# Attention of a cross-attention and expert layer: keys moved to the partitions, scores computed twice, work ordered by batch

## The chip, the cores and the metric

One NeuronCore of a Trainium2 chip. The metric is device time in microseconds (us) of one launch. All times here are of executions of the same program on the same inputs.

## What is computed

The input x has 4 batches of 512 tokens of width 128, the context 4 batches of 77 keys. The second half is a layer with eight experts, of which each token takes the two best. Cut to what matters:

```python
q = (layernorm(x) @ Wq + bq).reshape(b, nq, 16, 8).transpose(0, 2, 1, 3)
k = (ctx @ Wk + bk).reshape(b, nk, 16, 8).transpose(0, 2, 1, 3)
v = (ctx @ Wv + bv).reshape(b, nk, 16, 8).transpose(0, 2, 1, 3)
scores = jnp.where(mask, -jnp.inf, jnp.einsum('bhqd,bhkd->bhqk', q, k) / np.sqrt(8))
attn = jnp.einsum('bhqk,bhkd->bhqd', jax.nn.softmax(scores, -1), v)
x = x + attn.transpose(0, 2, 1, 3).reshape(b, nq, 128) @ Wo + bo
z = layernorm(x)
probs = softmax(z @ router_w + router_b)          # 9 choices: 8 experts, identity
gates = the two largest probs, 0 elsewhere
y = einsum('ebtf,efd->ebtd', gelu(einsum('btd,edf->ebtf', z, w1)), w2)
x = x + einsum('bte,ebtd->btd', gates[..., :8], y) + gates[..., 8:] * z
```

## The kernel before

Every instruction is placed by hand on its engine. Each engine runs its own list in order and waits on counting semaphores, so what stands behind a waiting instruction waits too. Everything is float32; a float32 product shows as two records on PE, a transpose as one. There are four parts.

1. **Start.** SP and ACT load the inputs. PE projects the keys (L724) and values (L728). DVE puts keys into kT and values into v_sb (L1019 to L1032). PE repeats V over the keys of all heads (L754), DVE masks it into vbd (L1139).
2. **Attention**, 16 tiles of 128 tokens, four in a batch, `n` the batch and `t` the tile. Tokens lie on the partitions, the 16 x 77 = 1232 keys of all heads on the free axis. For a tile, PE makes the scores in four groups of 32 rows (L774, four heads in each, 308 columns) into the four banks of ps_s. DVE reads each half of ps_s twice, for the maximum (L1058) and to subtract it (L1062). ACT takes the exponential of all 1232 columns (L665). PE transposes the result in ten chunks (L798), ACT copies them out (L547), and PE multiplies them with vbd (L807), 99 columns each; the row sums come along as a ninth column of each head. DVE divides by them (`weigh`, L1081, L1082), PE transposes (L782) and projects (L786), DVE adds the residual and takes statistics (`residual`, L1070 to L1076). The tiles overlap: the lists run `attend` of tile i-1 and `attn_t` of tile i-2 in step i.
3. **Router**, once a batch, within the steps of the next one: ACT normalizes (`norm2`, L591), PE transposes (L840) and makes the logits (L849), DVE picks the two best (`choose`, L1092 to L1107), PE counts the tokens of each expert (`ranks`, L861 to L867), DVE turns these into slots (`place`, L1116 to L1128), POOL sends the rows to DRAM by eight indirect DMAs (`send`, L480). The last batch is split in a part of three tiles and a part of one. Then DVE makes tables (from L1189), SP and ACT write padding rows, and SP waits for all sends.
4. **Experts**, 40 tiles of gathered rows: PE L917, L926 and L935, ACT L701, DVE L1208 to L1222, POOL L523. Then the pairs of results are added and stored.

Batches 1 and 2 are two rounds of a hardware loop, with registers in the waits; batches 0 and 3 are written out. The transposes' banks ps_t are taken in a numbered order of 18 "fills" a batch (`FILLS`, `ORDER`).

## Time and profile before

| | us |
|---|---|
| median of 3 timed runs | 253.03 (250.68 to 253.9) |
| span of the profiled execution | 257.3 |

The profiled execution has no time of its own beside its span. Its span is 4.3 us above the median of the timed runs, so it stands as its own time, and a sum made on it is brought to the median by taking 4.3 us off.

PE is busy for 191.6 us of the span, DVE 156.0, ACT 102.0, POOL 102.4. In the profile, L12 is line 12 of the kernel. PE is the matmul side of TensorE and PEld its weight loads. A row of a timeline gives start and duration in us, engine, line, operation, output and inputs, and count; in brackets stands how long the engine was idle before, and what released it. Ends of matmuls are modelled. PEclk is the granted share of TensorE's clock; where the trace holds no record of the clock, it shows as 1.00.

### The profile page before, as it was taken

The numbers are of one execution on the slowest core, as the hardware profiler recorded it, in microseconds if no ns is written. First come the engines' busy times: TensorE is split into PE (matmuls) and PEld (weight loads), VectorE is DVE, ScalarE is ACT, GpSimd is POOL, SyncE is SP. The second block draws the span as 40 slices with busy tenths as digits, with TensorE's granted clock in tenths as the row PEclk, the third lists the DMA queues.
The fourth block names the chain that finished last, engine by engine and source line by source line (L and its number), as shares of the span: only waits on it lengthen the run. The fifth ranks groups of instructions, "written<-read, shape, count | busy, mean of one in ns | idle before, by whom it ended". The sixth has DMA issues, their size and how long they took to land.

```text
span 257.3 us, 5658 instructions
## 1 busy us (share of the span) xinstructions
PE 191.6 (74%) x1467; PEld 169.9 (66%) x1468; DVE 156.0 (61%) x498; ACT 102.0 (40%) x210; POOL 102.4 (40%) x148
## 2 busy tenths in 40 slices
PE   1747899999986599849783200999999999999500
PEld 0516488778765587739782100899999999999500
DVE  2799968788883678938853650254554554554226
ACT  2411565678654476436653310122322322323100
POOL 8293001002047520782057479044554554554600
PEclk9999999999999589997978555599999999999955
DMA  3535892000001000110001031212222222210069
GB/s 98 159 122 215 263 309 83 4 0 0 4 20 44 9 0 0 37 36 0 0 28 50 21 103 50 61 47 74 59 68 64 71 62 68 62 52 11 3 218 271
DMA packets 20303, 18.30 MB, mean 71 GB/s; under 512 B 3255, under 2 KB 16752, under 8 KB 20287
## 3 DMA queue, kind: packets, MB, share of 16 engines
q1 hardware_dynamic: 16831, 13.98, 18.5%
q0 software_dynamic: 2304, 3.75, 4.7%
q10 hardware_dynamic: 1152, 0.37, 0.6%
q8 instruction: 8, 0.13, 0.2%
q14 instruction: 8, 0.07, 0.1%
HBM read 10.60 MB, written 8.50 MB: 74 GB/s over the span
## 4 chain that ended last, share of the span: by engine, by line
PE 48%; DVE 23%; issue 9%; DMA 6%; ACT 4%; another core or an unknown queue 4%; SPq 3%; POOL 1%; DVEq 0%; POOLq 0%; ACTq 0%
PE ps_s L926 14%; PE ps_av L807 8%; PE ps_av L935 7%; PE ps_o L935 6%; PE ps_t L798 5%; DVE mx L1058 4%; DVE sc L1062 3%; DMA pair_sb<-pairs 2%; PE ps_t L917 2%; DMA ctx_sb<-in_ctx 2%; DVE v_sb L1030 1%; PE ps_s L774 1%; DVE v_sb L1032 1%; SPq L317 1%
## 5 line engine op out<-in xcount | busy, mean ns | idle before, releaser
L523 POOL DMA_INDIRECT pairs<-yg,xg x40 | 39.1, 976 | 44.1 <-issue 22.7
L701 ACT ACTIVATE hT<-ps_s 128x512 f32<-128x512 f32 x40 | 23.9, 597 | 61.5 <-PE ps_s L926 61.5
L480 POOL DMA_INDIRECT slots<-rows,slot x32 | 31.7, 990 | 39.1 <-issue 18.3
L926 PE MATMUL ps_s<-xgT,w_now 128*128 128x128 f32 x320 | 44.4, 283 | 0.0
L807 PEld LDWEIGHTS ps_av<-vbd,exT 128*128 128x128 f32 x320 | 40.9, 205 | 2.4 <-issue 2.4
L807 PE MATMUL ps_av<-vbd,exT 128*128 128x99 f32 (+1 forms) x320 | 41.8, 286 | 0.8 <-issue 0.8
L926 PEld LDWEIGHTS ps_s<-xgT,w_now 128*128 128x128 f32 x320 | 40.5, 199 | 0.1
L1215 DVE COPY w_now<-w_sb 128x512 f32 x40 | 17.2, 429 | 21.5 <-issue 16.9
L798 PE MATMUL ps_t<-ident,ex 128*128 128x128 f32 x160 | 28.1, 314 | 0.1
L547 ACT COPY exT<-ps_t 128x384 f32<-128x384 f32 (+1 forms) x48 | 24.1, 514 | 7.5 <-PE ps_t L798 4.2
L1058 DVE TENSOR_REDUCE mx<-ps_s 128x8 f32<-128x616 f32 x32 | 25.4, 793 | 2.5 <-PE ps_s L774 1.9
L1062 DVE TENSOR_TENSOR sc<-ps_s,mx 128x616 f32<-128x616 f32 x32 | 25.6, 799 | 1.3
L665 ACT ACTIVATE ex<-sc 128x1232 f32<-128x1232 f32 x16 | 19.7, 1230 | 10.2 <-DVE sc L1062 10.1
L436 POOL TENSOR_TENSOR kbd<-kT,hm 128x308 f32<-128x308 f32 x4 | 2.8, 704 | 51.9 <-PE ps_s L774 46.8
L798 PEld LDWEIGHTS ps_t<-ident,ex 128*128 128x128 f32 x160 | 20.9, 160 | 2.6 <-ACT ex L665 0.8
L917 PE MATMUL ps_t<-ident,xg 128*128 128x128 f32 x40 | 11.5, 287 | 14.6 <-DMA xg<-slots 14.5
L935 PE MATMUL ps_av<-w_sb,hT 128*128 x160 | 22.2, 283 | 0.0
L935 PE MATMUL ps_o<-w_sb,hT 128*128 x160 | 21.5, 277 | 0.2 <-issue 0.2
L935 PEld LDWEIGHTS ps_av<-w_sb,hT 128*128 128x128 f32 x160 | 20.2, 198 | 0.2
L935 PEld LDWEIGHTS ps_o<-w_sb,hT 128*128 128x128 f32 x160 | 19.5, 192 | 0.4 <-issue 0.4
L774 PE MATMUL ps_s<-kbd,qT 32*128 32x308 f32 x128 | 16.7, 510 | 2.9 <-DVE sc L1062 1.6
L1208 DVE COPY xgT<-ps_t 128x128 f32<-128x128 f32 x40 | 11.4, 284 | 8.3 <-PE ps_t L917 8.3
(157 smaller groups left out, 239.9 us busy)
## 6 DMA issues: line engine op xcount, KB each, us to landing
xg<-slots SPq DMA_DIRECT2D x40, 65.0 KB
pairs<-zeros SPq DMA_DIRECT2D x4, 512.0 KB, 4.0
w_sb<-in_L_ffn_w SPq DMA_DIRECT2D x1, 2048.0 KB, 9.7
pair_sb<-pairs SPq DMA_DIRECT2D x3, 512.0 KB, 4.7
x_sb<-in_x SPq DMA_DIRECT2D x4, 256.0 KB, 6.7
out<-out_sb SPq DMA_DIRECT2D x3, 256.0 KB, 2.9
pairs<-yg,xg POOLq DMA_INDIRECT x40
slots<-rows,slot POOLq DMA_INDIRECT x32
```

Of the source, the lines that this page charges most:

```text
L480: pool.indirect_dma_start(slots, bass.IndirectOffsetOnAxis(ap=slot[k][:, t, c:c + 1], axis=0), rows[:, t, :], None, bounds_check=ROWS - 1, ...
L523: pool.indirect_dma_start(pairs, bass.IndirectOffsetOnAxis(ap=xg[:, u, D + 1:D + 2].bitcast(U32), axis=0), yg[:, u % 4, :], None, bounds_c ...
L547: act.copy(dst, src).then_inc(t_used, 1)
L665: act.activation(ex[:, t % 2, 0:HK], sc[:, t % 2, :], ACT.Exp).then_inc(ex_ready, 1)
L701: act.activation(hT[:, u % 2, :], ps_h[u % 2], ACT.Gelu).then_inc(h_used, 1)
L774: m = pe.matmul(ps_s[:, g, 0:GK], qT[r, P * t:P * (t + 1)], kbd[r, :, :].rearrange("p h k -> p (h k)"), start=True, stop=True)
L798: m = pe.transpose(ps_t[bank][:, P * (c - a):P * (c - a + 1)], ex[:, par, P * c:P * (c + 1)], ident[:, :])
L807: m = pe.matmul(ps_av[:, (DH + 1) * head0[c]:(DH + 1) * head0[c] + VC], exT[:, par, P * c:P * (c + 1)], v, start=c == 0, stop=c == NCH - 1 ...
L926: m = pe.matmul(ps_h[par][:, P * c:P * (c + 1)], w1_now[:, par, P * c:P * (c + 1)], xgT[:, par, :], start=True, stop=True)
L935: m = pe.matmul(ps_y[par], hT[:, par, P * c:P * (c + 1)], w2_sb[:, bass.ds(e + P * c, D)], start=c == 0, stop=c == FC - 1)
L1058: link(dve.tensor_reduce(m, s, AX.X, ALU.max))
L1062: dve.tensor_tensor(o.rearrange("p (g h k) -> p g h k", g=2, k=NK), s, m.rearrange("p (g h) -> p g h", g=2).unsqueeze(3) .to_broadcast([P, ...
```

## The change

Part 2 is written anew, and with it the order of parts 1 and 3. Part 4 is the same, but for the PSUM banks that it uses. The loop over batches is unrolled, and so are the registers in waits.

- **Scores twice.** The scores of a tile are made as before (`scores`, same shapes), but only for their maximum: DVE reads each half once (`maxima`) and puts the 16 maxima of a token into spare columns of mpad. After the four tiles of a batch, PE transposes mpad (`shifts_t`, four transposes), and DVE adds the maxima as extra rows to two masked copies of q (`shift_q`, two instructions of 512 columns), which POOL prepares (`own_q`). The second product (`scores_t`) has the keys on the partitions and 512 tokens on the free axis. Its stationary side kaug holds -1 in the extra rows, so that the product is the score less the maximum. The 308 keys of a group go in three pieces, of 128, 103 and 77 partitions, each with four products (one for each group of 32 rows) into the four banks of ps_s.
- **Exponential straight into place.** ACT takes it from PSUM, two banks (1024 columns) at a time, six times a batch (`exps`). Its output is the right-hand side of the next product: the ten transposes a tile and the copies exT are gone.
- **V stationary.** `attend` multiplies V (32 columns, one product for each of four column groups, 512 tokens) into ps_a, and a block of ones (`onest`) in the same way into ps_b, which gives the row sums on all partitions of a head: 24 products a batch. `weigh` is one reciprocal and one product of 128x512, and the result is already transposed for Wo: `attn_t` and its copy are gone.
- **By batch.** Projection, residual, statistics and normalization run once for 512 tokens. The router's part for batch n-2 runs in step n; the last batch isn't split. Scores of the next batch wait for the last exponentials, since ps_s is shared. The normalization and q of batch n+1 stand in front of the exponentials of batch n on ACT, those of batch 1 behind the exponentials of batch 0.
- **Start.** V is masked by two instructions of DVE instead of six; it is repeated only for the first two pieces (four products of PE in `spread_v`, two of them of 512 columns), and masked into vst and onest by six instructions (`spread`).

Cut to its core:

```diff
+    PIECE = [(NK, NK + P), (NK + P, GK), (0, NK)]
+    ROWSOF = [z - a for a, z in PIECE]
+    NC3 = len(PIECE)
+    SHIFT_ROW = 23
...
+            def spread_k(n):
+
+                k = kT[:, n * NK:(n + 1) * NK].unsqueeze(1).to_broadcast(by_block)
+                pool.tensor_tensor(kbd[:, n], k, hm4[:, :].unsqueeze(2).to_broadcast(by_block),
                                    ALU.mult).then_inc(kbd_ready, 1)
...
+            def shift_k(n):
+
+                pool.wait_ge(kbd_ready, n + 1)
+                pool.tensor_tensor(kaug[:, n], kbd[:, n], sm4[:, :].unsqueeze(2).to_broadcast(by_block),
+                                   ALU.subtract).then_inc(kaug_ready, 1)
+
+            def own_q(n):
+
+                pool.wait_ge(q_ready, n + 1)
+                if n >= 2:
+                    pool.wait_ge(sT_full, 6 * (n - 1))
+                pool.tensor_tensor(qa[n % 2][:, :], qT[n % 2][:, :], own_a[:, 0:1].to_broadcast([P, S]),
+                                   ALU.mult).then_inc(qown_ready, 1)
+                pool.tensor_tensor(qb[n % 2][:, :], qT[n % 2][:, :], hm4[:, 0:1].to_broadcast([P, S]),
+                                   ALU.mult).then_inc(qown_ready, 1)
...
+            def exps(n, c):
+
+                for pair in range(2):
+                    act.wait_ge(sT_full, n * 6 + c * 2 + pair + 1)
+                    if n > 0:
+                        act.wait_ge(av_full, (n - 1) * NC3 + c + 1)
+                    k = ROWSOF[c]
+                    act.activation(eT[c][0:k, 2 * pair:2 * pair + 2, :], ps_s[0:k, 2 * pair:2 * pair + 2, :],
+                                   ACT.Exp).then_inc(ex_ready, 1)
...
+                    norm2(n - 2)
+                    store_x2nT(n - 2)
+                if 0 < n < B - 1:
+                    store_xn(n + 1)
+                    store_xnT(n + 1)
+                    store_q(n + 1)
+                exps(n, 0)
+                exps(n, 1)
+                if n == 0:
+                    act.wait_ge(stats1_ready, B)
+                    seeds(seed1[:, TT:NT], mv1[:, TT:NT, 1], 2, seed1_ready)
+                if n >= 2:
+                    router_exp(n - 2)
+                exps(n, 2)
+                if n == 0:
+                    act.wait_ge(shift1_ready, 2)
+                    store_xn(1)
+                    store_xnT(1)
+                    store_q(1)
+                if n >= 1:
...
+            def spread_v():
+
+                pe.wait_ge(repeat_ready, 2)
+                pe.wait_ge(kT_ready, 1)
                 pe.wait_ge(v_ready, 1)
-                begin_fill(PRE_V)
...
+                for c, bank in enumerate((ps_a, ps_b)):
+                    k = ROWSOF[c]
+                    pe.matmul(bank[0:k, :], repeat[:, P * c:P * c + k], v_sb[:, :, :].rearrange("k b d -> k (b d)"),
+                              start=True, stop=True)
+                    i = pe.matmul(ps_m[1][0:k, B * c:B * (c + 1)], repeat[:, P * c:P * c + k], validT[:, :],
                                   start=True, stop=True)
...
+            def shifts_t(n):
+
+                if n == 0:
+                    pe.wait_ge(vr_used, 1)
+                if n >= 2:
+                    pe.wait_ge(x2nT_ready, n - 1)
+                pe.wait_ge(s_used, (n + 1) * TT * 2)
+                for t in range(TT):
+                    i = pe.transpose(ps_m[1][:, P * t:P * (t + 1)], mpad[:, t, :], ident[:, :])
+                i.then_inc(mT_full, 1)
+
+            def scores_t(n, c):
+
+                a, z = PIECE[c]
+                q = (qb if c == 2 else qa)[n % 2]
+                if c == 0:
+                    pe.wait_ge(kaug_ready, n + 1)
+                    pe.wait_ge(aug_ready, 2 * n + 2)
+                for pair in range(2):
+                    if c > 0 and pair == 0:
+                        pe.wait_ge(ex_ready, n * 6 + 2 * c)
+                    for g in (2 * pair, 2 * pair + 1):
+                        r = slice(32 * g, 32 * g + 32)
+                        m = pe.matmul(ps_s[0:z - a, g, :], kaug[r, n].rearrange("p h k -> p (h k)")[:, a:z], q[r, :],
+                                      start=True, stop=True)
+                    m.then_inc(sT_full, 1)
+
+            def attend(n, c):
+
+                k = ROWSOF[c]
+                if c == 0:
+                    if n == 0:
+                        pe.wait_ge(vr_used, 2)
+                    else:
+                        pe.wait_ge(at_ready, n)
+                pe.wait_ge(ex_ready, n * 6 + 2 * c + 2)
+                for g in range(G):
+                    r = slice(32 * g, 32 * g + 32)
+                    pe.matmul(ps_a[r, :], vst[0:k, c, n * D + 32 * g:n * D + 32 * g + 32], eT[c][0:k, g, :],
+                              start=c == 0, stop=c == NC3 - 1)
+                for g in range(G):
+                    r = slice(32 * g, 32 * g + 32)
+                    m = pe.matmul(ps_b[r, :], onest[0:k, c, n, :], eT[c][0:k, g, :], start=c == 0,
+                                  stop=c == NC3 - 1)
+                m.then_inc(av_full, 1)
+
+            def project(n):
+
+                pe.wait_ge(aug_ready, 2 * n + 4 if n + 1 < B else 2 * n + 2)
+                if n == B - 1:
+                    pe.wait_ge(x2nT_ready, n)
+                pe.wait_ge(at_ready, n + 1)
+                for t in range(TT):
+                    i = pe.matmul(ps_m[1][:, D * t:D * (t + 1)], attnT[:, P * t:P * (t + 1)], wo_sb[:, :],
+                                  start=True, stop=True)
+                i.then_inc(o_full, 1)
...
+            for n in range(B):
+                if n > 0:
+                    scores(n, 0)
+                    attend(n - 1, 2)
+                scores(n, 1)
+                scores(n, 2)
+                if n >= 2:
+                    norm2_t(n - 2)
+                if 0 < n < B - 1:
+                    norm1_t(n + 1)
+                scores(n, 3)
+                if 0 < n < B - 1:
+                    project_q(n + 1)
+                if n >= 2:
+                    logits(n - 2)
+                shifts_t(n)
+                scores_t(n, 0)
+                if n > 0:
+                    project(n - 1)
+                scores_t(n, 1)
+                attend(n, 0)
+                if n >= 2:
+                    ranks(n - 2)
+                scores_t(n, 2)
+                attend(n, 1)
+                if n == 0:
+                    norm1_t(1)
+                    project_q(1)
+            attend(B - 1, 2)
+            norm2_t(B - 2)
+            logits(B - 2)
+            project(B - 1)
+            ranks(B - 2)
+            norm2_t(B - 1)
+            logits(B - 1)
+            ranks(B - 1)
...
+            def spread(c, values, own):
+
+                k = ROWSOF[c]
+                head = piecehead[0:k, c, :]
+                dve.tensor_tensor(vst[0:k, c, :].rearrange("p (x j d) -> p x j d", j=HG, d=DH),
+                                  values.rearrange("p (x j d) -> p x j d", j=HG, d=DH),
+                                  head.unsqueeze(1).unsqueeze(3).to_broadcast([k, B * G, HG, DH]), ALU.mult)
+                return dve.tensor_tensor(onest[0:k, c, :, :].rearrange("p b (j d) -> p b j d", d=DH),
+                                         own.unsqueeze(2).unsqueeze(3).to_broadcast([k, B, HG, DH]),
+                                         head.unsqueeze(1).unsqueeze(3).to_broadcast([k, B, HG, DH]), ALU.mult)
...
+            def maxima(n, t):
+
                 for half in range(2):
...
+                    if n > 0 and t == 0 and half == 0:
+                        dve.wait_ge(mT_full, n)
+                    dve.tensor_reduce(mpad[:, t, :].rearrange("p (g r) -> p g r", g=G)
+                                      [:, 2 * half:2 * half + 2, SHIFT_ROW:SHIFT_ROW + HG],
+                                      ps_s[:, 2 * half:2 * half + 2, 0:GK].rearrange("p g (h k) -> p g h k", k=NK),
+                                      AX.X, ALU.max).then_inc(s_used, 1)
+
+            def shift_q(n):
+
+                dve.wait_ge(mT_full, n + 1)
+                dve.wait_ge(qown_ready, 2 * n + 2)
+                dve.scalar_tensor_tensor(qa[n % 2][:, :], ps_m[1][:, :], shift_a[:, 0:1], qa[n % 2][:, :],
+                                         ALU.mult, ALU.add).then_inc(aug_ready, 1)
+                dve.scalar_tensor_tensor(qb[n % 2][:, :], ps_m[1][:, :], sm4[:, 0:1], qb[n % 2][:, :],
+                                         ALU.mult, ALU.add).then_inc(aug_ready, 1)
+
+            def weigh(n):
+
+                dve.wait_ge(av_full, NC3 * (n + 1))
+                link(dve.reciprocal(inv[:, :], ps_b[:, :]))
+                if n > 0:
+                    dve.wait_ge(o_full, n)
+                dve.tensor_tensor(attnT[:, :], ps_a[:, :], inv[:, :], ALU.mult).then_inc(at_ready, 1)
...
+            maxima(0, 0)
+            dve.wait_ge(piece_ready, 3)
+            spread_all()
+            for n in range(B):
+                for t in range(TT):
+                    if n > 0 or t > 0:
+                        maxima(n, t)
+                shift_q(n)
+                if n == 0:
+                    for b in range(1, B):
+                        stats1(b)
                     refine1(slice(TT, NT), 2)
-                    spread_v()
-                if t == 2 and kind == "first":
-                    dve.wait_ge(xb_ready, B)
-                if t == 3 and kind != "first":
-                    choose(n - 1)
-                if kind != "first" or t >= 2:
-                    i_ = residual(i - 2, (t + 2) % 4)
-                    if t == 1:
-                        i_.then_inc(stats_ready, 1)
-                if kind != "first" or t >= 1:
-                    weigh(i - 1, (t + 1) % 2)
-                if t == 1 and kind != "first":
+                    constants()
+                if n > 0:
+                    weigh(n - 1)
+                if n >= 2:
+                    choose(n - 2)
+                if n > 0:
+                    residual(n - 1)
+                if n >= 2:
+                    place(n - 2)
+                if n > 0:
                     refine2(n - 1)
-                if t == 3 and kind != "first":
-                    place(n - 1)
-
-            def steps():
-                for t in range(TT):
-                    step("first", 0, t)
-                chain_at = chain.local
-                with dve.Fori(1, B - 1) as n:
-                    chain.enter(n - 1, LINKS)
-                    for t in range(TT):
-                        step("mid", n, t)
-                    chain.leave(B - 2)
-                for t in range(TT):
-                    step("last", B - 1, t)
-
-            steps()
-            residual(NT - 2, 2).then_inc(stats_ready, 1)
+            weigh(B - 1)
+            choose(B - 2)
+            residual(B - 1)
+            place(B - 2)
             refine2(B - 1)
-            weigh(NT - 1, 1)
-            residual(NT - 1, 3).then_inc(stats_ready, 1)
             choose(B - 1)
-            refine2(B)
             place(B - 1)
```

**PE, a tile of batch 1 or 2 before**: scores, transpose of the attention, transposes of the exponentials in ps_t, projection, products with vbd.

```order
L774 MATMUL ps_s<-kbd,qT 128x308 x4
L782 MATMUL ps_o<-ident,av 128x128
L798 MATMUL ps_t<-ident,ex 128x128 x7
L786 MATMUL ps_o<-wo_sb,avT 128x128
L798 MATMUL ps_t<-ident,ex 128x128 x3
L807 ISA
L807 MATMUL ps_av<-vbd,exT 128x99
```

The last row comes ten times, with register instructions between. **PE now, in the step of batch 2**, from the transposed product of its first piece on (kaug the keys with the extra rows, eT the exponentials, vst and onest V and the ones):

```order
L664 MATMUL ps_m<-ident,mpad 128x128 x4
L679 MATMUL ps_s<-qa,kaug 128x512 x4
L709 MATMUL ps_m<-wo_sb,attnT 128x128 x4
L679 MATMUL ps_s<-qa,kaug 103x512 x4
L694 MATMUL ps_a<-eT,vst 32x512 x4
L698 MATMUL ps_b<-eT,onest 32x512 x4
```

The projection of the batch before stands between the first and the second piece. Ahead of it, in the same step, stand the scores of the four tiles and what was placed between them:

```order
L652 MATMUL ps_s<-kbd,qT 128x308 x4
L694 MATMUL ps_a<-eT,vst 32x512 x4
L698 MATMUL ps_b<-eT,onest 32x512 x4
L652 MATMUL ps_s<-kbd,qT 128x308 x8
L718 MATMUL ps_m<-ident,rows_0 128x128 x4
L615 MATMUL ps_m<-ident,xn_sb 128x128 x4
L652 MATMUL ps_s<-kbd,qT 128x308 x4
L621 MATMUL ps_m<-xnT,wq_sb 128x512
L729 MATMUL ps_m<-wr_sb,x2nT 128x64 x4
```

The two transposes, of batch 0's normalized rows and batch 3's, stand ahead of the fourth tile's scores, which wait behind them. **DVE now, in the step of batch 2**, from the maxima to the start of choosing:

```order
L960 TENSOR_REDUCE mpad<-ps_s 128x2x4 x8
L969 SCALAR_TENSOR_TENSOR qa<-ps_m,shift_a,qa 128x512
L971 SCALAR_TENSOR_TENSOR qb<-ps_m,sm,qb 128x512
L977 RECIPROCAL inv<-ps_b 128x512
L980 TENSOR_TENSOR attnT<-ps_a,inv 128x512
L1005 TENSOR_TENSOR lgx<-ps_m,rb_sb 128x4x9
```

The eight reductions stand alone, without the subtractions between them. The reciprocal and the product behind it are ahead of what PE needs for the projection.

## Rows read from the trace of the kernel before

**Rows 1.** Busy time by stretch: start, attention (two), its end, tables and sends.

```profile
core 0: us, PE busy (x) PEld busy (x) DVE busy (x) ACT busy (x) POOL busy (x), PEclk, DMA share, GB/s
0.00:46.00 46.00, 32.26 (x178) 23.89 (x183) 35.16 (x100) 18.64 (x38) 16.24 (x45) 1.00 0.57 175
46.00:71.00 25.00, 24.17 (x208) 19.88 (x205) 21.09 (x69) 18.54 (x41) 1.52 (x4) 1.00 0.01 2
71.00:125.90 54.90, 44.37 (x340) 38.05 (x339) 39.60 (x107) 30.56 (x64) 24.10 (x33) 0.91 0.05 17
125.90:147.70 21.80, 10.32 (x70) 8.80 (x68) 11.79 (x82) 9.07 (x29) 10.26 (x11) 0.73 0.09 29
147.70:161.70 14.00, 0.68 (x2) 0.42 (x3) 4.11 (x16) 1.28 (x1) 11.24 (x16) 0.50 0.26 74
```

**Rows 2.** Waits: engine and line, released by: us in total, times, longest.

```profile
DVE rsum L1081 <- remote: 9.9, 2, 5.9
```

**Rows 3.** The chain that ended last, in order of time: start, us, what.

```profile
80.26 5.39 another core or an unknown queue
...
110.65 4.01 another core or an unknown queue
...
156.18 1.57 DMA slots<-padrows
```

**Rows 4.** Groups by line and shape, DVE: busy us, mean ns, idle before.

```profile
L1062 DVE TENSOR_TENSOR sc<-ps_s,mx 128x616 f32<-128x616 f32 x32 | 25.6, 799 | 1.3
L1058 DVE TENSOR_REDUCE mx<-ps_s 128x8 f32<-128x616 f32 x32 | 25.4, 793 | 2.5 <-PE ps_s L774 1.9 <-issue 0.3
...
L1032 DVE TENSOR_SCALAR v_sb<-v_sb,validT 77x128 f32<-77x128 f32 x4 | 7.3, 1879 | 0.0
...
L1081 DVE RECIPROCAL rsum<-ps_av 128x16 f32<-128x16 f32 x16 | 3.9, 243 | 14.7 <-remote 9.9 <-PE ps_av L807 4.5
...
L1019 DVE SCALAR_TENSOR_TENSOR kT<-ps_av,bk_sb,valid 128x308 f32<-128x308 f32 x1 | 0.5, 504 | 0.0
...
L1117 DVE RECIPROCAL lsum<-lsum 128x3 f32<-128x3 f32 x1 | 0.2, 176 | 0.0
```

**Rows 5.** Groups by line and shape, ACT.

```profile
L547 ACT COPY exT<-ps_t 128x384 f32<-128x384 f32 x32 | 15.3, 478 | 6.2 <-PE ps_t L798 3.0 <-remote 1.9 <-issue 0.2
...
L547 ACT COPY exT<-ps_t 128x512 f32<-128x512 f32 x16 | 9.4, 586 | 1.3 <-PE ps_t L798 1.1
```

**Rows 6.** Timeline, PE: query projection (first, at the start), scores, products.

```profile
12.58 2.05 PE L742 MATMUL ps_t<-xnT,wq_sb 128*128 128x512 f32 x2 [0.77 <-ACT xnT L547]
...
43.27 1.05 PE L742 MATMUL ps_t<-xnT,wq_sb 128*128 128x512 f32 x2
...
48.22 2.37 PE L807 MATMUL ps_av<-vbd,exT 128*128 x20
50.52 0.80 PE L774 MATMUL ps_s<-kbd,qT 32*128 32x308 f32 x8
```

**Rows 7.** Timeline, DVE and ACT: first and last of choose, of place; a normalization.

```profile
65.56 0.19 DVE L1092 TENSOR_TENSOR lgx<-lg_sb,rb_sb 128x36 f32<-128x36 f32 x1
...
67.50 0.20 DVE L1107 TENSOR_TENSOR lgx<-lgx,top 128x44 f32<-128x44 f32 x1
...
69.30 0.18 DVE L1116 TENSOR_REDUCE lsum<-lex 128x4 f32<-128x36 f32 x1
...
70.45 0.23 DVE L1128 TENSOR_REDUCE slot<-prod 128x8 uint32<-128x72 f32 x1
...
75.43 1.63 ACT L565 ACTIVATE xn_sb<-x_sb,shift,rstd 128x128 f32 x4
```

**Rows 8.** Timeline, the sends' last stretch and the first expert product.

```profile
144.66 0.97 POOL L480 DMA_INDIRECT slots<-rows,slot  x1 [3.85 <-ACT rows L577]
...
153.78 0.97 POOL L480 DMA_INDIRECT slots<-rows,slot  x1 [0.30 <-issue]
...
161.74 0.42 PE L926 MATMUL ps_s<-xgT,w_now 128*128 128x128 f32 x1
```

821 lines of the change are left out of this document (288 added, 533 removed).

## The prediction

> **What bounds the kernel now.** I read busy time by stretch first [rows 1]. The reader is to see that DVE is busy for 21.1 of the 25 us of batch 1 (46 to 71) and PE for 24.2: both are near their limit there. In the next 54.9 us, two batches, both have slack (39.6 and 44.4), and the list of waits [rows 2] shows part of why: DVE waited twice, 9.9 us together, for a semaphore whose sender the profile doesn't know. The chain that ended last has the same two places, 5.39 and 4.01 us [rows 3]. In both, products were done by the record and their signal came late. I call these 9.4 us the late signals. Without them a batch takes 23 to 25 us, set by DVE with PE close behind. After the attention come 21.8 us in which no engine is busy for more than 12: a chain of small steps for the last batch's router; then 14.0 us of tables and sends, and the experts.
>
> **Durations.** They come from one profiled execution, whose span is 257.3 us; the median of the runs shown is 253.0, so a sum on the span loses 4.3 at the end.
> - DVE: maximum of a half 0.79, subtraction of a half 0.80 [rows 4]. A two-source instruction of 512 columns: from 504 ns at 308 columns and 793 to 799 at 616, some 0.95 ns a column, so 0.70 us.
> - ACT: a copy takes 478 ns for 384 columns and 586 for 512 [rows 5], 0.84 ns a column, so an exponential of 1024 columns 1.02 us. Four normalizations take 1.63 [rows 7].
> - PE: the query projection of 512 columns is two records and takes 1.05 with its fill [rows 6]; I take 0.44 a record. The 20 products of 128 by 99 take 2.37, so about 0.11 a record of some 100 to 128 columns. The eight records of the scores, 308 columns in four row groups, take 0.80; one after another they would be 8 x 0.26 = 2.1. So row groups run side by side, and a transposed product of four row groups, 512 columns, is 2 x 0.44 + 0.2 = 1.1.
> - Choosing takes 2.1 from its first to its last row, placing 1.4 [rows 7]. Residual and statistics for 512 tokens I put at 2.2 (0.7, and eight short instructions like those of choosing), the four chained steps of the second normalization at 0.8 after their seed.
>
> **Two prices that no row shows.** The reciprocal of 128x512: the trace has 176 ns for 3 columns and 243 for 16 [rows 4], so 5.2 ns a column. Bounds: 0.7 us, if the 16 columns are slow only for their stride and it runs like other instructions, and 3.8, if the longest of the 16 (0.26) sets the slope. I take 0.18 + 509 x 0.0052 = 2.9, the line through both rows. The Trainium skill, VectorE: DVE Perf Modes, section on the fixed hardware budget, says that the reciprocal is an iterative divide with a repeat count of 8. At its 0.96 GHz and eight cycles an element that would be an estimated 4.3 us, and the sum would be 5 us longer; the slope of the rows is below it, so the trace doesn't fully agree.
>
> The product of four column groups (`attend`): no row has any. If they run side by side as row groups do, 2 x 2 x 0.44 + 0.2 = 2.0 us for both banks; if one after another, 16 x 0.44 = 7.0. I take 2.0, since the row groups are the nearest row. The Trainium skill, TensorE: Matmul & The Clock Gate, part 3, states 2.38 times for three column groups of 512 columns; by it `attend` would be an estimated 2.2 to 2.4 us and hidden nearly as well. No row here shows it.
>
> **Part by part.** Removed: 32 subtractions, 25.6 us of DVE; 160 transposes of exponentials on PE and 48 copies on ACT; 16 exponentials give way to 24 of 1.02. Added for a batch: two instructions of shifting, 1.4 on DVE; the reciprocal, 2.9, and its product, 0.7; twelve transposed products, 3.3 on PE; 24 stationary-V products, 6.0. DVE then has 6.4 + 1.4 + 3.6 + 2.1 + 2.2 + 1.4 + 1.0 = 18.1 a batch and PE some 18, below the 21.1 and 24.2 of batch 1 now. But all four banks of ps_s serve the scores, the transposed pieces and the exponentials in turn, so the step is a chain. I follow it from the end of the first exponential of the last piece of a batch (0):
> - Second exponential to 1.0, seeds 0.6, last DVE steps 0.8: DVE is free at 2.5. Four tiles of maxima, 1.6 each, with two gaps of 0.4 to 0.6 for scores behind `attend`: to 9.9.
> - Transposes of maxima 0.6, `shift_q` 1.4: 12.1. The first transposed product to 13.2, its exponentials hidden behind DVE's `weigh`: 12.1 + 2.9 + 0.7 = 15.7. Projection of the batch before, eight records: 16.7. Only then the second piece, which stands behind it on PE: first pair at 17.5, exponentials to 19.6, `attend` (2.0) and ranks to 20.1, third piece, first exponential ended at 22.0.
>
> So the step of batch 3 is 22.0. Batch 2 has two transposes ahead of its fourth scores, and the second of them needs 1.65 of normalization on ACT behind the copy of the first: the fourth maximum ends at 12.9 and the logits at 13.4, so +3.3: 25.3. Batch 1, without router work, is 20.4.
>
> Start: scores of tile 0 as now, at 15.7 to 17.1. The 11 us of DVE for V (7.3 of it four slow instructions [rows 4]) are gone, but PE's repeat of V on a cold clock (two products of 512 columns; a pair took 2.05 there [rows 6]) goes to 20.9, masking to 24.0, three tiles to 29, shifts to 31.8, three pieces of 3.1 with a cold first product to 41.4. Then, uncovered, normalization 1.65, transposes, copy, q and its copy for batch 1: first scores at 46.5, against 45.9 now. What was saved is given back here.
>
> Three steps end at 46.5 + 20.4 + 25.3 + 22.0 = 114.2. The tail is 1.0 + 2.0 (last `attend`) + 3.7 (`weigh`) + 2.1 + 2.2 + 1.4 + 1.2 for batch 2's choosing and the last residual, then 1.65 + 0.6 + 0.6 + 1.1 + 2.1 + 1.4 and handovers: 21.4. Last placing at 135.6, 12.1 us ahead of 147.7.
>
> Of that, 3 go in the sends. Batch 2's placing ends at 126.7, its eight sends last 8 x 1.30 [rows 8], then rows are copied (0.9), then batch 3's eight: 148.4. Now the pads land last, at 157.75 [rows 3], and the first expert product starts 4.0 later [rows 8]; on that scale it starts at 152.5 with its landing, 9.2 ahead of 161.7. The experts are the same.
>
> **Sum.** 257.3 - 9.2 = 248.1. Add 2 for a cold clock after the idle stretch at 41 to 46: two products at 2.05 in place of 1.05 [rows 6], no row has more. This has no late signal, while the trace now has 9.4 us of them. Since I know no cause, bounds are 0 and 9.4; I take 5, near the middle, as both places lie beside POOL's sends, which stay. 248.1 + 2 + 5 = 255.1, less 4.3: **250.7 us**, 0.9% below the median, which a measurement of this kernel can hardly tell from no change; the bound is about 2% (248.0 and 258.1).
>
> **Rivals.**
> A. Faster: no late signals, or a cheap reciprocal. For it: the loop with registers in waits is gone, and both late signals lie in batches 2 and 3. Without them 245.7. With a reciprocal of 0.7, PE gets its projection 2.2 earlier, 1.6 of it in each of three steps and 2.2 in the tail: -7, 243.7. The Trainium skill, Runtime: NRT & Kernel Launch, on instruction fetch, says that taken branches break prefetching, which unrolling ends; no wait in these rows can be put to it. Against: batch 3, written out, has a late signal too.
> B. Slower by the chain: all late signals stay (+4.4), and each of the four reciprocals costs 0.9 more (+3.6): 258.7.
> C. Slower, by one mechanism: column groups don't run side by side. The place is `attend`, three times a batch, where PE has 2.1 us of exponentials to hide it. Two at a time it takes 3.7: +1.7 on the second scores, +1.4 on the third piece, +2 on the next batch's first scores, so +5 a batch, 271. One at a time 7.0: +14 a batch, 305. It decides from about 2.4 us on. Against it are the row groups [rows 6].
>
> **Chances.** Forecast, 246 to 256: 0.47; A: 0.28; B: 0.11; C: 0.14. The range leaves out the deep end of A and most of C: 240 to 263. A gives nearly all of faster (0.28), and the forecast's lower edge 0.05 more: 0.33. Slower is C, and 0.10 of B: 0.24. The rest, 0.43, is within 2%.
>
> **What would show it.** Right: steps of 20, 25 and 22 us between the first scores of batches; the reciprocal near 2.9; sixteen records of `attend` in 2.0 to 2.4; the second piece's product starting behind the projection; POOL sending without a pause to the end. Wrong: `attend` over 3; maxima of batch 1 well before 45; DVE without idle time in a step, for then DVE, not the chain, sets it; or placing of the last batch at 148 or later.

## The result, and the profile after

| | us |
|---|---|
| before, 4 timed runs | 253.47 (250.68 to 255.58) |
| after, 4 timed runs | 274.49 (271.72 to 276.47) |
| ratio | 1.088, 95% interval 1.078 to 1.099 |
| span of the profiled execution of after | 269.9 |

Slower by 8.8%, where 250.7 with a range of 240 to 263 was forecast. The times are medians of all runs, while the ratios here and below leave out the slower of a kernel's runs, which lie some 1.5% above its fastest. First the page: the share of busy time in 40 slices of 6.7 us.

```profile
PE   1756495993986769875961400199999999999600
...
DVE  2887720257342394588388280145454545455226
...
PEclk9995577557795556995985555589999999999955
```

The row to read is PEclk. The attention fills slices 1 to 23, and in nearly half of them TensorE had half its clock for most of the slice (5 is 1.2 GHz; 9 is 0.9 or more of 2.4). PE and DVE both have slack beside it. By stretch (start of kernel, batches 1, 2 and 3, tail to the last placing, tables and sends, experts; the last two numbers are the clock and the DMA share, then GB/s):

```profile
core 0: us, PE busy (x) PEld busy (x) DVE busy (x) ACT busy (x) POOL busy (x), PEclk, DMA share, GB/s
0.00:47.10 47.10, 26.93 (x126) 11.23 (x127) 24.11 (x85) 14.14 (x26) 18.26 (x44) 0.79 0.37 119
47.10:76.10 29.00, 23.62 (x124) 8.89 (x124) 13.51 (x22) 8.45 (x12) 4.07 (x4) 0.64 0.29 85
76.10:109.40 33.30, 25.95 (x146) 11.09 (x142) 17.12 (x51) 11.38 (x21) 3.82 (x6) 0.64 0.00 1
109.40:133.20 23.80, 18.31 (x134) 8.28 (x134) 16.93 (x51) 7.73 (x15) 10.94 (x17) 0.86 0.06 20
133.20:157.40 24.20, 10.17 (x68) 6.58 (x60) 14.40 (x71) 6.79 (x18) 18.71 (x24) 0.64 0.11 37
157.40:175.10 17.70, 0.75 (x3) 0.49 (x4) 4.92 (x17) 1.28 (x1) 14.10 (x22) 0.50 0.24 68
175.10:252.00 76.90, 76.74 (x665) 75.84 (x665) 38.56 (x116) 23.30 (x40) 36.74 (x38) 0.99 0.22 58
```

Against [rows 1]: in batches 1 and 2 the granted clock is 0.64, DVE is busy for 13.5 of 29.0 and 17.1 of 33.3 us, so no engine's work sets the length, the chain does. The experts are as long as before. The two groups of DVE that matter (busy us, mean ns of one | idle us before them, and what ended it):

```profile
L960 DVE TENSOR_REDUCE mpad<-ps_s 128x8 f32<-128x616 f32 x32 | 24.2, 794 | 24.3 <-PE ps_s L652 24.2
...
L977 DVE RECIPROCAL inv<-ps_b 128x512 f32<-128x512 f32 x4 | 13.4, 3350 | 0.8 <-PE ps_b L698 0.8
```

The 32 maxima cost what they did [rows 4], but DVE waited 24.3 us for their scores. The reciprocal of 128x512 takes 3.35 us. The chain of waits through batch 1 (start us, us, what):

```profile
47.14 1.41 PE ps_s L652 x8
48.55 1.86 PE ps_a L694 x8
50.42 1.71 PE ps_b L698 x8
...
58.85 2.00 PE ps_m L621 x2
...
63.00 3.27 DVE inv L977
...
67.14 2.04 PE ps_m L709 x8
69.19 1.98 PE ps_s L679 x8
71.17 1.17 PE ps_a L694 x8
72.34 0.86 PE ps_b L698 x8
```

The names: ps_s L652 are scores, ps_a L694 and ps_b L698 the two banks of `attend`, ps_m L621 the query projection, inv the reciprocal, ps_m L709 the output projection, ps_s L679 a transposed product. At the full clock, in the same trace or in [rows 6], scores take 0.80, a bank 0.86 to 1.0, a transposed product 1.1 and a query projection 1.05. Here they take 1.41, 1.86 and 1.71, 1.98 and 2.00. Only from 71 on are they short again, and after the next waits (82 to 105) long once more.

### The profile page after: what moved, and what is told of

Its sections match the earlier page's. It is cut to its first block, busy times and chain, and to the rows that moved or that the text cites. A ratio compares the mean times of both kernels' runs of the same rounds, so it can differ in the third digit from the quotient of the medians.

```text
span 269.9 us, 4784 instructions
## 1 busy us (share of the span) xinstructions
PE 184.5 (68%) x1262; PEld 124.0 (46%) x1263; DVE 135.9 (50%) x422; ACT 73.7 (27%) x128; POOL 109.5 (41%) x154
## 4 chain that ended last, share of the span: by engine, by line
PE 60%; DVE 14%; issue 8%; DMA 6%; POOL 5%; ACT 4%; SPq 1%; POOLq 0%; DVEq 0%; ACTq 0%
PE ps_s L811 13%; PE ps_s L652 7%; PE ps_a L820 7%; PE ps_b L820 6%; PE ps_s L679 5%; PE ps_a L694 5%; DVE inv L977 5%; POOL slots L400 4%; PE ps_b L698 4%; PE ps_m L709 3%; PE ps_m L621 3%; DVE mpad L960 2%; DMA pair_sb<-pairs 2%; PE ps_m L802 2%; DMA ctx_sb<-in_ctx 2%
## 5 line engine op out<-in xcount | busy, mean ns | idle before, releaser
L400 POOL DMA_INDIRECT slots<-rows,slot x32 | 31.5, 985 | 35.7 <-issue 23.3
L510 ACT ACTIVATE eT<-ps_s 128x1024 f32<-128x1024 f32 (+2 forms) x24 | 23.2, 1018 | 55.2 <-PE ps_s L679 55.2
L960 DVE TENSOR_REDUCE mpad<-ps_s 128x8 f32<-128x616 f32 x32 | 24.2, 794 | 24.3 <-PE ps_s L652 24.2
L1103 DVE COPY w_now<-w_sb 128x512 f32 x40 | 18.0, 449 | 21.2 <-issue 17.1
L652 PE MATMUL ps_s<-kbd,qT 32*128 32x308 f32 x128 | 21.8, 616 | 8.5 <-DVE mpad L960 6.8
L802 PE MATMUL ps_m<-ident,xg 128*128 128x128 f32 x40 | 11.5, 287 | 18.5 <-DMA xg<-slots 18.3
L820 PE MATMUL ps_a<-w_sb,hT 128*128 x160 | 21.5, 277 | 0.0
L820 PE MATMUL ps_b<-w_sb,hT 128*128 x160 | 21.5, 277 | 0.1
L679 PE MATMUL ps_s<-qa,kaug 32*128 32x512 f32 (+1 forms) x64 | 14.7, 1000 | 8.4 <-DVE qb L971 6.4
L820 PEld LDWEIGHTS ps_b<-w_sb,hT 128*128 128x128 f32 x160 | 19.5, 192 | 0.3 <-issue 0.3
L820 PEld LDWEIGHTS ps_a<-w_sb,hT 128*128 128x128 f32 x160 | 19.4, 192 | 0.3
L652 PEld LDWEIGHTS ps_s<-kbd,qT 32*128 32x128 f32 x128 | 9.4, 237 | 21.5 <-DVE mpad L960 13.5
L694 PE MATMUL ps_a<-eT,vst 128*32 128x512 f32 (+2 forms) x96 | 16.0, 748 | 0.2 <-ACT eT L510 0.2
L709 PE MATMUL ps_m<-wo_sb,attnT 128*128 128x128 f32 x32 | 8.2, 437 | 8.4 <-DVE attnT L980 8.4
L698 PE MATMUL ps_b<-eT,onest 128*32 128x512 f32 (+2 forms) x96 | 13.8, 651 | 0.0
```

The lines of the kernel that those rows point to most:

```text
L400: pool.indirect_dma_start(slots, bass.IndirectOffsetOnAxis(ap=slot[k][:, t, c:c + 1], axis=0), rows[:, t, :], None, bounds_check=ROWS - 1, ...
L510: act.activation(eT[c][0:k, 2 * pair:2 * pair + 2, :], ps_s[0:k, 2 * pair:2 * pair + 2, :], ACT.Exp).then_inc(ex_ready, 1)
L652: m = pe.matmul(ps_s[:, g, 0:GK], qT[n % 2][r, P * t:P * (t + 1)], kbd[r, n].rearrange("p h k -> p (h k)"), start=True, stop=True)
L679: m = pe.matmul(ps_s[0:z - a, g, :], kaug[r, n].rearrange("p h k -> p (h k)")[:, a:z], q[r, :], start=True, stop=True)
L694: pe.matmul(ps_a[r, :], vst[0:k, c, n * D + 32 * g:n * D + 32 * g + 32], eT[c][0:k, g, :], start=c == 0, stop=c == NC3 - 1)
L698: m = pe.matmul(ps_b[r, :], onest[0:k, c, n, :], eT[c][0:k, g, :], start=c == 0, stop=c == NC3 - 1)
```

## The experiments

Each was timed beside the kernel before on the same chip. That kernel took 252.66 us beside the first four, 252.31 beside the next four, 251.28 beside `e_order_warm`, `e_early`, `e_nomax` and `e_all`, and 252.72 beside the last two; across these groups the ratios are the thing to compare. Edits are to the changed kernel unless said. Since stretches without a record count as 1.00, the granted clock of a whole run is a rough sign. The lengths of the products on the chain are the measure.

### The clock, the order, the reciprocal

**The changed kernel again**, as the measure of its group.

> The changed kernel as it is, as the measure for the three below on the same chip. Every theory: 272 to 277 us, first scores of batches 1, 2 and 3 some 29 and 33 us apart, granted clock 0.75 to 0.80, each reciprocal of 128x512 at 3.35 us.

Measured: 275.2 us (before: 252.66), ratio 1.091 (1.079 to 1.104), clock 0.744. In its profile the first scores of batch 1 start at 50.1 in place of 47.1; the steps of batches 1, 2 and 3 are 29.5, 30.9 and 26.0. One of its other runs shows a clock of 0.832 and still took 272.96 us.

**Filler products** (`e_warm`):

```diff
+            def warm(bank, columns):
+                for c in range(0, columns, 512):
+                    w = min(512, columns - c)
+                    pe.matmul(bank[:, 0:w], wq_sb[:, :], x_sb[:, 0:w], start=True, stop=True)
...
                 shifts_t(n)
+                warm(ps_s[:, 0], 640)
                 scores_t(n, 0)
                 if n > 0:
+                    warm(ps_m[1], 1280)
                     project(n - 1)
...
                 if n == 0:
+                    warm(ps_m[1], 1536)
                     norm1_t(1)
+                    warm(ps_m[1], 384)
                     project_q(1)
+                    warm(ps_m[1], 256)
```

> Adds products that nobody reads, into banks that are free, where TensorE waits: 640 columns before the first transposed product of a batch, 1280 before each projection of the batch before, and 2176 around batch 1's normalization. Theory 'clock' (the half clock is the largest part of the miss): products on the chain at 2.05 us in place of 1.05 cost about 20 us in all; with most of it at the full clock the time is 260 to 266 us and the granted clock over 0.9. Theory 'order' (the chain is long through waits, and the clock fell beside them at no cost): 272 to 277 us, with the clock up all the same. If the fillers themselves get in the way it is over 277.

Measured: 262.05 us, ratio 1.043 (1.033 to 1.052), 13.2 us below the changed kernel of the same group, with more work on PE. The granted clock was 0.869, short of the 0.9 expected, and even that holds a stretch without a record: before 49 us it shows as 1.00, while the products for V took 2.00 and 1.87 (1.05 and 0.94 at the full clock in after). From the first scores of batch 1 to the last placing the clock was 0.83 against 0.65 in the repeat of the changed kernel, and that part took 98.9 us in place of 110.5. The chain of this run, at the places of the fence above, and at the place where the clock had fallen all the same:

```profile
49.20 0.80 PE ps_s L657 x8
50.00 1.00 PE ps_a L699 x8
50.99 0.86 PE ps_b L703 x8
...
65.37 1.13 PE ps_m L714 x8
...
83.77 2.02 PE ps_m L621 x2
...
86.55 1.97 PE ps_m L734 x8
```

The scores take 0.80, `attend` 1.00 and 0.86, the projection 1.13 in place of 2.04. The last two rows lie in the half-clock stretch of batch 2, where no filler stands. So theory 'clock' holds: nothing was moved or taken away, and 13.2 of the 22.5 us lost against the kernel before are back (12 by the two ratios).

**Projection later** (`e_order`):

```diff
                 scores_t(n, 0)
-                if n > 0:
-                    project(n - 1)
                 scores_t(n, 1)
+                if n > 0:
+                    project(n - 1)
                 attend(n, 0)
```

> On TensorE the projection of the batch before stands behind the second transposed product, not ahead of it. Theory 'order': in each of three batches the second product starts when the exponentials of the first piece end, 2.9 us earlier (66.3 in place of 69.1), so 266 us, and a little less if the shorter wait keeps the clock up. Theory 'clock': the wait for the reciprocal only moves to another place, the products stay at the half clock, 272 us or more.

Measured: 274.44 us, ratio 1.094 (1.085 to 1.103): nothing. The timeline of PE in batch 1 shows where the gain went:

```profile
66.74 2.05 PE L679 MATMUL ps_s<-qa,kaug 32*103 32x512 f32 x8 [2.02 <-ACT eT L510]
...
68.72 2.08 PE L709 MATMUL ps_m<-wo_sb,attnT 128*128 128x128 f32 x8
...
70.73 1.94 PE L694 MATMUL ps_a<-eT,vst 128*32 128x512 f32 x8
...
76.54 1.02 PE L652 MATMUL ps_s<-kbd,qT 32*128 32x308 f32 x8
```

The second transposed product does start when the exponentials end, at 66.74. But from there to the next batch's first scores PE is busy without a pause, mostly at the half clock, and the projection has only changed its place in that row: it is 13.2 us from the reciprocal's start (63.35) to 76.54, as 13.1 in the changed kernel.

**Division left out** (`e_norecip`): `dve.tensor_copy(inv, ps_b)` in place of `dve.reciprocal(inv, ps_b)`; the output is not divided by the row sums.

> Leaves the division out: a copy of 512 columns, about 0.7 us, stands for the reciprocal of 3.35. Theory 'reciprocal on the chain': 2.7 us less in each of four places, 264 us. Theory 'reciprocal hidden behind the exponentials': only the last counts, 271 us. Below 262 the shorter wait must also have kept TensorE's clock up.

Measured: 264.9 us, ratio 1.050 (1.041 to 1.059), 10.3 below the changed kernel. The copy took 0.68 us in place of 3.35, and 4 x 2.67 = 10.7: the reciprocal lies on the chain in all four places, as the prediction had it. The clock was 0.761, and the products of batch 1 stayed long (its first bank took 1.94 with its fill, as in after), so this gain and that of the fillers are of two kinds.

### The kernel before: its late signals, its loop, its start

**The kernel before again** (`before_again`), for a second profile.

> The kernel before once more, for a second profile. Theory 'late signals are of the kernel': the chain shows two waits of VectorE for an unknown sender again, 9 us together, and the span stands at 257. Theory 'of that execution': they are absent or elsewhere, and the span is some us shorter than 257.3.

Measured: 252.2 us, ratio 1.003 (0.997 to 1.009), span 252.1. No wait has an unknown sender. Yet the maxima of batches 2 and 3 begin at 71.23 and 102.88: batch 2 takes 31.6 us, as long as in the first profile (31.0), where such a wait of 5.9 us lay in it. Its chain runs through GpSimd, which the late signal had hidden:

```profile
83.50 0.98 POOL slots L480
...
86.48 1.26 POOL base_sb L497
...
88.43 1.22 ACT rows L591 x3
...
89.69 1.11 PE ps_t L840 x4
```

The eight sends of batch 0 and the identity part follow one another on POOL to 87.7; only then may ACT overwrite the rows (L591), and the transposes behind it are followed by the scores of the last tile on PE. Batches 0 to 2 share these buffers there; in the changed kernel batches take two sets in turn, and its list of waits has no wait of ACT for them.

**The loop written out** (`e_unroll`, an edit to the kernel before):

```diff
...
-            with eng.Fori(1, B - 1) as n:
+            for n in range(1, B - 1):
                 for t in range(TT):
                     step("mid", n, t)
...
-            with pool.Fori(1, B - 1) as n:
+            for n in range(1, B - 1):
...
-                with dve.Fori(1, B - 1) as n:
-                    chain.enter(n - 1, LINKS)
+                for n in range(1, B - 1):
...
-                    chain.leave(B - 2)
```

> The kernel before with the loop over its two middle batches written out, and nothing else. Theory 'loop': the late signals come from the loop, and 3 to 9 us go: 244 to 250 us. Theory 'nothing': 253 us, within 1%; then nothing of the change's result is due to its being unrolled.

The lines left out keep the numbering of the fills right. Measured: 248.18 us (before 252.31), ratio 0.990 (0.984 to 0.996): faster by 1.0%, between the two theories. Batch 2, from first maximum to first maximum, took 28.4 us in place of 31.6.

**V masked by two-source instructions** (`e_vfix`, an edit to the kernel before):

```diff
-            dve.tensor_copy(v_sb[:, :, :, DH], validT[:, :].unsqueeze(2).to_broadcast([NK, B, H]))
-            for b in range(B):
-                i = dve.tensor_scalar(v_sb[:, b, :, 0:DH], v_sb[:, b, :, 0:DH], validT[:, b:b + 1], None, ALU.mult)
-            i.then_inc(v_ready, 1)
+            valid_h = validT[:, :].unsqueeze(2).to_broadcast([NK, B, H])
+            dve.tensor_tensor(v_sb[:, :, :, DH], valid_h, valid_h, ALU.mult)
+            dve.tensor_tensor(v_sb[:, :, :, 0:DH], v_sb[:, :, :, 0:DH],
+                              validT[:, :].unsqueeze(2).unsqueeze(3).to_broadcast([NK, B, H, DH]),
+                              ALU.mult).then_inc(v_ready, 1)
```

> The kernel before, with the copy and the four one-source multiplications of V (3.72 and 7.27 us) made one two-source multiplication each, as the changed kernel does with V. Theory 'the start is VectorE's': the first maximum comes about 9 us earlier, 244 us. Theory 'something else is late next' (the scores of tile 0 are done at 17, the tile of V at 20): 3 to 6 us less, 247 to 250.

Measured: 248.26 us, ratio 0.990 (0.986 to 0.994), as the second theory has it. The timeline of DVE:

```profile
13.69 0.68 DVE L1032 TENSOR_TENSOR v_sb<-v_sb,validT 77x512 f32<-77x512 f32 x1
...
18.44 1.25 DVE L1043 CAST jot<-jot_i 128x40 f32<-128x40 int32 x1
...
19.67 1.23 DVE L1046 CAST ebase<-ebasei 128x9 f32<-128x9 int32 x1
...
21.12 1.00 DVE L1049 COPY nextrow<-ebase 128x9 f32<-128x9 f32 x1
22.16 0.80 DVE L1059 TENSOR_REDUCE mx<-ps_s 128x8 f32<-128x616 f32 x1
```

The statistics behind these instructions begin at 14.3, 6 us earlier than in the profile of before. But what comes next now falls where POOL adds a bias to x (17.2 to 22.1), and three small one-source instructions of 9 and 40 columns stretch to 1 us or more each, while their neighbours of the same kind take 0.15. In the repeat of the kernel before they come later, at 24.4, and take 0.16 to 0.18. The first maximum is at 22.16 against 25.19: 3 us of the 6.

**Both** (`e_vfix_unroll`, on the kernel before).

> Both edits of the two runs above on the kernel before. Expected: the two gains added, 241 to 249 us; if the loop costs nothing, the same as with V alone.

Measured: 245.04 us, ratio 0.978 (0.972 to 0.983). The gains add. This is the fastest version of all: 2.2% below the kernel before, and 10% below the changed one by their ratios.

### How much of the rest is order

**Later projection with fillers** (`e_order_warm`): the edits of `e_order` and `e_warm`, with 512 columns in place of 1280.

> The later projection of e_order with the fillers of e_warm (only 512 columns, not 1280, stand between the first and the second transposed product). In e_order TensorE at the half clock was busy without a pause from the second product to the end of the batch, so the order bought nothing. Theory 'clock first, then order': at the full clock the second product starts 2.0 us earlier in three batches (64.5 in place of 66.5 in e_warm), 6 us below e_warm, 256 us. Theory 'order never counts': 261 to 263. If the smaller filler lets the clock fall: over 265.

Measured: 258.93, 263.22, 263.71 and 263.86 us (before 251.28), median 263.46. This spread is as wide as the gain that was looked for, so the times don't settle whether the order counts at the full clock. The profile, of the run of 263.22, shows a part of it: from the first scores of batch 1 to the last placing it took 96.3 us in place of the 98.9 of `e_warm`. Batch 1 got shorter, 50.41 to 71.44 in the chain, 21.0 in place of 23.3 us; batch 2 did not. There the first transposed product took 1.99, in `e_warm` 1.14, though the same filler stands ahead of it in both; why the clock was low there is open.

**Batch 1 normalized earlier** (`e_early`):

```diff
                 exps(n, 0)
-                exps(n, 1)
                 if n == 0:
                     act.wait_ge(stats1_ready, B)
                     seeds(seed1[:, TT:NT], mv1[:, TT:NT, 1], 2, seed1_ready)
+                exps(n, 1)
+                if n == 0:
+                    act.wait_ge(shift1_ready, 2)
+                    store_xn(1)
...
                 scores_t(n, 2)
+                if n == 0:
+                    norm1_t(1)
                 attend(n, 1)
                 if n == 0:
-                    norm1_t(1)
                     project_q(1)
```

> The changed kernel with batch 1's normalization on ScalarE ahead of the last exponentials of batch 0, and its transposes ahead of the second product with V. Expected by the chain of after (first scores of batch 1 at 47.1, of which 3.2 are the normalization and its transposes after the exponentials): 3 us less, 271 to 272 us. Theory 'clock': with less of a pause TensorE also keeps its clock into batch 1 and it is 265 to 269. Rival, the time comes back in the next step: 274 to 276.

Measured: 266.56 us, ratio 1.061 (1.052 to 1.070), the 265 to 269 of theory 'clock': a move worth 3 us of chain gave some 8. The scores of batch 1 ran at the full clock (0.80 us for eight records). They began no earlier in that profile, at 48.66, for its start was slower: the products for V took 2.00 and 1.87 there.

**Maxima left out** (`e_nomax`): no calls of `scores` and `maxima`, so no maximum is subtracted.

> Leaves out the scores with tokens on partitions, their 32 maxima and with them the subtraction (the shift is zero): the price of computing the scores twice. Theory 'the chain is as long as its parts': from the first scores of a batch to its shift are some 12 us, 9 of them four tiles of scores and maxima, so four times 9 to 12 less, 225 to 240 us. Rival 'something else bounds then' (GpSimd's 32 sends at 1.28, ScalarE's exponentials, the half clock): 245 to 260.

Measured: 250.6 us, ratio 0.994 (0.989 to 1.000). The theory of parts falls, the rival stands: computing the scores twice costs 24 us, not 35 or more. The clock of the profiled run was 0.791, so this is a price mostly at the half clock; at the full clock it wasn't measured. Batch 2 of this run took 29.4 us from one reciprocal to the next (49.80 to 79.21) against 32.1, for with the four tiles gone another chain has their place (ACT and PE in turn):

```profile
65.30 1.66 ACT rows L519 x4
67.00 1.11 PE ps_m L721 x4
...
68.72 1.55 ACT xn_sb L487 x4
...
72.17 2.09 PE ps_m L620 x2
74.28 0.70 ACT qT L499
75.02 1.97 PE ps_m L732 x8
```

12 us of hand-overs, 65.3 to 77.0: rows of batch 0 for the router, then the normalization, transposes, projection and q of batch 3, logits, and only behind them on PE the transposes for the shift.

**Everything that moves work** (`e_all`): fillers (512 and 512 columns), later projection, earlier normalization.

> Fillers, later projection and earlier normalization of batch 1 together: the best that the changed kernel gives by moving work alone. Expected if the gains add (13 for the clock, 6 for the order at the full clock, 3 for the start): 253 us, level with the kernel before. Rival: the parts overlap, 256 to 261.

Measured: 259.47 us (before 251.28), ratio 1.036 (1.025 to 1.047): the rival. The gains overlap.

**More fillers** (`e_warm2`), with 896 columns ahead of batch 3's `norm1_t`, 384 ahead of the logits there and 896 ahead of the last projection; and the same **with the earlier normalization** (`e_warm2_early`). They were run because the chain of `e_warm` still shows the half clock in batch 2.

> e_warm with three more fillers: 896 columns between batch 0's router transposes and the transposes of batch 3's normalization, 384 before the logits there, 896 before the last projection. In e_warm the clock was still at half in most of 80 to 96, with the query projection at 2.0, the logits at 1.97 and half clock scores in the chain. Theory 'clock': 4 to 6 us of it are left, 256 to 258. Theory 'ScalarE's copies and normalizations make that chain, the clock stands beside it': 261 to 262.

> The fillers of e_warm2 and the earlier normalization of e_early, with the projection in its first place. Theory 'the gains add' (e_early alone took 8 us, of which 3 are its own chain and 5 clock that e_warm has already): 3 us below e_warm2, 253 to 255. Rival: GpSimd's sends make the end (16 of them between the placing of batch 2 and the end of the last), and it stays within 1 us of e_warm2.

Measured: 261.74 us, ratio 1.036 (1.025 to 1.046), and 259.2 us, ratio 1.029 (1.022 to 1.036), beside 252.72. By its time `e_warm2` falls where the second theory has it (261 to 262). Its profile, of its slowest run, shows both: batch 2 was 3.3 us shorter than in `e_warm` (26.3 against 29.6 between reciprocals), as theory 'clock' has it, but the clock was at half at the start (0.50 from 24 to 33) and batch 3 was 1.4 longer; where it falls is not the same from run to run. `e_warm2_early` came out 2.5 below `e_warm2`, and not in the 253 to 255 expected; the intervals of the two ratios overlap, so this step between them is not shown by the times. In its profile the three batches had the full clock nearly throughout (0.93, 1.00 and 1.00), so it shows their chain without the clock. The 1.00 of its first row stands for a stretch without a record (the products for V took 2.01 and 1.87), and its tail had 0.71:

```profile
0.00:47.70 47.70, 31.76 (x138) 14.51 (x139) 23.73 (x85) 13.96 (x26) 18.27 (x44) 1.00 0.37 120
47.70:70.90 23.20, 21.12 (x136) 8.30 (x138) 13.50 (x22) 8.61 (x13) 4.07 (x4) 0.93 0.35 102
70.90:97.10 26.20, 23.48 (x158) 10.23 (x158) 16.84 (x51) 11.26 (x21) 3.34 (x6) 1.00 0.00 1
97.10:118.40 21.30, 19.28 (x140) 8.84 (x144) 16.87 (x51) 7.57 (x14) 11.22 (x16) 1.00 0.07 23
118.40:143.10 24.70, 12.23 (x76) 7.45 (x67) 13.46 (x71) 6.87 (x18) 18.87 (x24) 0.71 0.12 37
143.10:160.80 17.70, 0.69 (x2) 0.43 (x3) 4.88 (x17) 1.28 (x1) 14.11 (x22) 0.50 0.24 68
```

The last placing ends at 143.1, 1.3 us ahead of the 144.4 in the repeat of the kernel before, and the span is still 257.1 against 252.1. Of that, 4.0 us are there at the first expert product (160.8 against 156.8), and they come from GpSimd's sends; the last 1.0 lies in the experts. The sends (first to last start, after, the kernel before again, and `e_warm2_early`):

```profile
L400 POOL DMA_INDIRECT slots<-rows,slot x32: 966/975/1162, 108.4 to 168.8; - x32
```

```profile
L480 POOL DMA_INDIRECT slots<-rows,slot x32: 967/975/1163, 74.4 to 150.5; - x32
```

```profile
L400 POOL DMA_INDIRECT slots<-rows,slot x32: 966/977/1162, 96.6 to 154.5; - x32
```

In the kernel before the last send starts 6.1 us after the last placing. In both others it starts 11.4 after it. In all three the last 16 sends run nearly back to back from the placing of batch 2 on, 19.4 us from first to last start before, and 20.9 now, with a copy of the rows between them. The rest of the difference is when they can begin: 13.3 us ahead of the last placing before (131.1 against 144.4), and only 9.5 now (147.9 against 157.4, and 133.7 against 143.1), since the router's part for batch 2 stands in the tail. That makes 1.5 and 3.8 of the 5.3 us.

## Why the prediction was wrong

The points are those of the forecast's sum; after's own trace, and the run whose three batches had the full clock beside it. Its earlier normalization shortens the chain ahead of batch 1's first scores, and its fillers lengthen it.

| | forecast | after | after again | `e_warm2_early` |
|---|---|---|---|---|
| first scores of batch 1 | 46.5 | 47.1 | 50.1 | 47.7 |
| step of batch 1 | 20.4 | 29.0 | 29.5 | 23.2 |
| batch 2 | 25.3 | 33.3 | 30.9 | 26.2 |
| batch 3 | 22.0 | 23.8 | 26.0 | 21.3 |
| tail, to the last placing | 21.4 | 24.2 | 24.1 | 24.7 |
| to the first expert product | 16.9 | 17.7 | 17.6 | 17.7 |
| first expert product | 152.5 | 175.1 | 178.3 | 160.8 |

- **The step that failed: "Add 2 for a cold clock."** It priced the half clock as two products after the idle stretch at 41 to 46, because the trace of before has little of it. Between the last column and that of after lie 14.3 us, seven times that: 15.4 in the steps of the three batches, less 1.1 elsewhere. `e_warm`, which only adds fillers, gave back 13.2. The rows to see it by were there: in the kernel before PE had half its clock in a query projection of the start [rows 6] and in the tail, where it was busy for 10.3 of 21.8 us [rows 1], and the forecast itself made the step a chain in which PE waits for DVE or ACT two or three times a batch. PE's busy time of 18 us a batch was worked out at the full clock, while here the clock turned on what PE did before (`e_warm`). The Trainium skill, TensorE: Matmul & The Clock Gate, part 1, puts the penalty of the ramp at under 1% of a typical kernel's span. That is said of a ramp, and this trace shows more than one: the clock fell again in every batch, and fillers alone were worth 5% (`e_warm`).
- **The column groups** (rival C): right in the mechanism that was weighed, and C is false. Both banks take 1.86 us at the full clock (1.00 and 0.86 in `e_warm`), where 2.0 was forecast from the row groups. But at the half clock they took 3.57 (1.86 and 1.71 in batch 1), over the 3 named as a sign of being wrong and near the 3.7 at which C was priced: what C feared for `attend` came about, by the clock, and that the measured 274.5 lies near C's 271 is luck. The 2.2 to 2.4 worked out from the Trainium skill, TensorE: Matmul & The Clock Gate, part 3, was too much; the trace decides.
- **The reciprocal**: mis-sized. 2.9 was taken, with 3.8 as the upper bound; it measured 3.35, so the columns cost 6.2 ns and not 5.2. The upper bound, from the longest of the small ones, was nearer. Being on the chain in four places (shown by `e_norecip`), it made 1.8 us of the miss. The 4.3 worked out from the Trainium skill, VectorE: DVE Perf Modes, section on the fixed hardware budget, was too much by 0.95; the trace decides here too.
- **The chain**: right in kind, and its sizes hold to 1 us in batches 2 and 3 at the full clock. Batch 1 was 2.8 too short: `attend` of the second piece (1.9) stands on PE ahead of the next batch's first scores, the reciprocal took 0.45 more, and the query projection 1.67 in place of 1.05. That is read from the chain, and not tested alone. The tail of `e_warm2_early` was 3.3 longer than forecast and not at the full clock: its last four transposes took 1.12 and its last logits 1.94, where the same records took 0.66 and 1.08 some 13 us before, together 1.3; the filler ahead of its last projection held that up by 1.8 (125.6 to 127.46), and the reciprocal made 0.5.
- **The late signals**: the reading of before was wrong. They were taken as 9.4 us of its length, and 5 were added to the forecast. A second profile has none, and its batch 2 is as long; GpSimd's sends and identity part bound it. The changed kernel has none either, and rival A's premise, that a batch takes 23 to 25 us without them, falls for batch 2. The 5 us also hid a part of the miss: without them the forecast was 245.7. That the unrolled loop is worth something was right, and worth 1.0%.
- **The sends**: "3 go in the sends" measured 17.7 - 14.0 = 3.7 against the first profile, where the pads landed last. Against the repeat, where the sends alone make that end (12.4 from the last placing to the first product), it is 5.3.
- **The sum of the miss**: at the first expert product after stands 22.6 behind the forecast. The 7 added for the signals and the cold clock, and 0.8 less behind that point, leave 14.8 between the span of 269.9 and the sum's 255.1. The other 8.9 are between span and median: the 4.3 taken off belonged to one execution of the kernel before, while after's median lies 4.6 above the span of its profiled execution. Two sums are a little off as they stand: 255.1 less 4.3 is 250.8, and 14 a batch on top of 250.7 is 307, not C's 305.
- **The range**: it covered the known unknowns (reciprocal, column groups, signals) but the clock, an unknown of its own, had no rival. A rival 'the chain runs at the half clock' would have stood at 263 (250.7 less the 2, plus the 14.3 above, a number known only now), the very edge of the range, before any term that was too short.
- **What was saved at the start** was given back, as forecast, and more. The 47.1 looks like a hit against 46.5 but is partly luck: the forecast had PE's repeat of V on a cold clock, and in this execution its two pairs took 1.05 and 0.94. In the repeat they took 2.01 to 2.07, as forecast, and the first scores of batch 1 came at 50.1, 3.6 late; the transposed products and `attend` behind them ran at the half clock too (2.05 and 1.87).

## What to carry to other kernels

A change that turns overlapped work into a chain is to be priced with TensorE at the clock that the chain will grant it: sum the products on the chain at both levels of the clock, and let the half clock be a rival with its own chance wherever the new order makes PE wait in every step. Look for small pieces inside a change that can stand alone: here the masking of V and the unrolling gave 2.2% on the old kernel, while the whole rewriting, which has both in it, lost 9%. And read a stall of one execution in a second profile before it is credited to anything; another engine may be just as late behind it.
